# One addition over four PSUM banks in place of four: the output tiles of a steady MLP unit

## The reference, cut to what matters

```python
cms_out  = gelu(attn_out @ cW1 + cb1) @ cW2 + cb2 + target_embed      # 512 -> 2048 -> 512
concat   = concatenate([attn_out, cms_out], axis=-1)
modifier = gelu(concat @ mW1 + mb1) @ mW2 + mb2                       # 1024 -> 2048 -> 512
out      = clip(x + cms_out + modifier, 0.0, 1.0)
```

## Time and profile before

| | us |
|---|---|
| median of 3 runs | 1183.29 |
| lowest and highest of them | 1183.22, 1184.39 |
| span of the profiled execution, first to last instruction | 1181.1 |
| PE busy in it | 1150.9 (97%) |
| DVE busy | 617.0 (52%) |
| ACT busy | 348.1 (29%) |
| POOL busy | 225.0 (19%) |
| PE's granted clock, mean | 0.993 |

### The profile page before, as it was taken

One profiled execution on the slowest core, in us unless ns is written; L12 is line 12 of the kernel. 1 busy time (PEld: TensorE's weight loads), 2 busy tenths in 40 slices (PEclk: granted clock), 3 DMA queues, 4 the chain that ended last, 5 costly groups with the idle time before them and its releaser, 6 DMA issues.

```text
span 1181.1 us, 14411 instructions
## 1 busy us (share of the span) xinstructions
PE 1150.9 (97%) x5201; PEld 954.2 (81%) x5201; DVE 617.0 (52%) x943; ACT 348.1 (29%) x611; POOL 225.0 (19%) x158
## 2 busy tenths in 40 slices
PE   7999999999999999999899999999999999999993
PEld 6888888788888888888788888888888888888883
DVE  4334344266656566665963444444444444344866
ACT  4333333322232232322421221221212212213554
POOL 2303113110110110110911111101001111113355
PEclk9999999999999999999999999999999999999997
DMA  5011000000010010010000000000000000001522
GB/s 179 1 37 36 0 36 18 18 25 30 18 36 18 18 36 18 18 36 27 27 27 27 27 27 26 1 27 27 27 27 27 27 27 27 27 14 59 152 81 89
DMA packets 41671, 41.33 MB, mean 35 GB/s; under 512 B 2165, under 2 KB 28841, under 8 KB 41641
## 3 DMA queue, kind: packets, MB, share of 16 engines
q1 hardware_dynamic: 41640, 40.93, 11.0%
HBM read 36.73 MB, written 4.19 MB: 35 GB/s over the span
## 4 chain that ended last, share of the span: by engine, by line
PE 90%; DVE 4%; ACT 2%; POOL 2%; DMA 1%; issue 1%; SPq 0%; POOLq 0%; ACTq 0%; DVEq 0%
PE bank L416 30%; PE bank L418 30%; PE bank L417 30%; PE bank L428 1%; DVE stats L944 1%; POOL res L382 1%; DMA raw<-W_up_dram 0%; POOL cms_lo L351 0%; DMA Wk_raw<-Wk_dram 0%; DVE z_odd L942 0%; DVE z_even L942 0%; DVE z_even L931 0%; POOL wsplit L351 0%; ACT gelu_f L738 0%; ACT wsplit L739 0%
## 5 line engine op out<-in xcount | busy, mean ns | idle before, releaser
L861 DVE TENSOR_TENSOR res<-bank,res 128x512 f32<-128x512 f32 x240 | 163.9, 691 | 261.3 <-PE bank L418 261.3
L680 ACT ACTIVATE gelu_f<-bank,hidden_bias 128x512 f32<-128x512 f32 x128 | 88.3, 690 | 636.3 <-PE bank L418 636.1
L351 POOL TENSOR_TENSOR wsplit<-raw,wsplit 128x512 fp32r<-128x512 f32 (+1 forms) x64 | 100.8, 1576 | 717.9 <-ACT wsplit L607 717.9
L861 DVE TENSOR_TENSOR cms_acc<-bank,cms_acc 128x512 f32<-128x512 f32 x240 | 163.4, 691 | 121.7 <-PE bank L418 121.7
L416 PE MATMUL bank<-attn_hi,wsplit 128*128 128x512 f32 x512 | 200.0, 391 | 3.1 <-DVE cms_lo L868 3.1
L416 PE MATMUL bank<-gelu_hi,wsplit 128*128 128x512 f32 x512 | 199.3, 389 | 0.8 <-DVE gelu_lo L847 0.8
L418 PE MATMUL bank<-attn_hi,wsplit 128*128 128x512 f32 x512 | 199.8, 390 | 0.0
L417 PE MATMUL bank<-attn_lo,wsplit 128*128 128x512 f32 x512 | 199.8, 390 | 0.0
L418 PE MATMUL bank<-gelu_hi,wsplit 128*128 128x512 f32 x512 | 199.2, 389 | 0.0
L417 PE MATMUL bank<-gelu_lo,wsplit 128*128 128x512 f32 x512 | 199.2, 389 | 0.0
L416 PE MATMUL bank<-cms_hi,wsplit 128*128 128x512 f32 x288 | 113.2, 393 | 2.9 <-DVE z_even L942 1.8
(11 more groups left out here) (131 smaller groups left out, 1287.6 us busy)
## 6 DMA issues: line engine op xcount, KB each, us to landing
raw<-cW_dram SPq DMA_DIRECT2D x32, 256.0 KB, 2.8
raw<-mW_dram SPq DMA_DIRECT2D x16, 512.0 KB, 4.2
x_raw<-x_dram SPq DMA_DIRECT2D x4, 1024.0 KB, 5.3
raw<-mW_dram SPq DMA_DIRECT2D x16, 256.0 KB, 4.4
raw<-W_down_dram SPq DMA_DIRECT2D x4, 512.0 KB, 3.8
raw<-W_up_dram SPq DMA_DIRECT2D x4, 512.0 KB, 4.7
out_dram<-z_even SPq DMA_DIRECT2D x8, 256.0 KB, 2.0
out_dram<-z_odd SPq DMA_DIRECT2D x8, 256.0 KB, 2.0
```

What stands on the lines that cost most here:

```text
L351: pool.tensor_tensor(dst, src, f32(hi), ALU.subtract).then_inc(done, 1)
L680: act.activation(dst[:, g, :], bank[r][:, :], ACT.Gelu, bias=hidden_bias[:, s:s + 1]).then_inc(gelu_made, 1)
L861: op = dve.tensor_tensor(dst, src, dst, ALU.add)
```

## The change

The PSUM tensors `bank[4]` to `bank[7]` become one tensor `outs` of 128 x 4 x 512, of which they are now slices. A steady `add_unit` (no start of an accumulator) waits once, for the fourth output tile, and adds all four tiles with one 128x2048 instruction, which raises `summed` by 4. The first four units of each MLP keep their four instructions.

```diff
-        bank = [ctx.enter_context(nc.psum_tensor(f"bank{i}", [P, 512], F32)) for i in range(8)]
+        bank = [ctx.enter_context(nc.psum_tensor(f"bank{i}", [P, 512], F32)) for i in range(4)]
+        outs = ctx.enter_context(nc.psum_tensor("outs", [P, KT, 512], F32))
+        bank += [outs[:, m, :] for m in range(KT)]
...
             def add_unit(i, r, total, start=None):
 
+                if start is None:
+                    dve.wait_ge(out_filled, i * 4 + KT)
+                    dve.tensor_tensor(total[:, r, :, :], outs[:, :, :], total[:, r, :, :], ALU.add).then_inc(summed, KT)
+                    return
                 for m in range(KT):
                     dst, src = total[:, r, m, :], bank[4 + m][:, :]
                     dve.wait_ge(out_filled, i * 4 + (m + 1))
                     if start == "cms":
                         op = dve.tensor_scalar(dst, src, cms_bias[:, r, m:m + 1], None, ALU.add)
-                    elif start == "mod":
+                    else:
                         if m == 0:
                             dve.wait_ge(res_added, KT * (r + 1))
                         op = dve.scalar_tensor_tensor(dst, src, bias[:, MB2 + m:MB2 + m + 1], dst, ALU.add, ALU.add)
-                    else:
-                        op = dve.tensor_tensor(dst, src, dst, ALU.add)
                     op.then_inc(summed, 1)
```

## The result

The changed kernel takes 1229.4 us (median of 4 runs, 1229.2 to 1229.9) against 1183.3 us: 46.1 us slower, a ratio of 1.0383 with a 95% interval of 1.0369 to 1.0398. The forecast was 1224 us, the range 1207 to 1242. The profiled execution took 1229.2 us with a span of 1227.4, so 1.8 us lie around the span here; the forecast had taken 2.2.

What follows compares the result with a forecast made beforehand. PE was taken to bound the kernel, other engines counting only where they make it wait. Terms 34.0 + 2.8 + 2.4 + 0 + 1.6 = 40.8 us on a span of 1181.1 gave 1224 us, range 1207 to 1242.

Steps and rivals of the forecast that it cites:

- What bounds, and the chain: Whole kernel: PE bounds, busy 97% of the span; in steady cms units low(i+1) follows the addition, out(i+1) follows low(i+1).
- Part 1 and 2: Steady addition: waiting for the fourth tile loses 2.04 us of cover; one 2048-element instruction takes 2.29 us.
- Part 3: Steady cms units: each 0.43 to 0.62 us over 5.44, in sum 34.0 us up to out(60).
- Part 4: Between the MLPs: hidden(64) 2.8 us later, then 2.4 us of wait at hidden(66).
- Part 5: Mod units: nothing lost, 7.2 us of addition chain hidden within a unit of 8.16 us.
- Part 6: End of the kernel: the chain from add(126) on ends 1.6 us later.
- the clock stayed at 1.00: Rival on steady cms units: PE's clock falls after each of 56 gaps, 95 us more, 1320 us; chance 0.04.
- the addition ran at the single rate: Rival: the wide addition runs at double rate, 1.43 us, and fits the slack, 1185 us; chance 0.04.
- merging did save its fixed costs: Rival: nothing saved by merging, wide addition 2.76 us, 0.47 more in 56 units, 1250 us; chance 0.06.

Runs made afterwards that it cites:

- low-first: Changed kernel with DVE making the low part of unit i ahead of the wide addition of unit i-1 in the cms MLP: 1192.0 us, ratio 1.0065.
- four late additions: Changed kernel with its one 128x2048 addition replaced by four 128x512 additions behind the same single wait for the fourth tile: 1238.9 us, ratio 1.0466.
- the turns: Kernel before, with GpSimd's additions of batch r into res waiting until cms_lo of batch r-1 is done: 1179.9 us, ratio 0.9974; rerun 1180.0 us.
- mod-only: Changed kernel with the wide addition kept in the second (mod) MLP only, the steady cms additions narrow again: 1186.5 us, ratio 1.0019.
- changed kernel with turns: Changed kernel with GpSimd's additions of batch r into res waiting until cms_lo of batch r-1 is done: 1223.7 us, ratio 1.0344.

## Why the prediction was right, and what it sized wrongly

- **What bounds, and the chain** (fourth tile, wide addition, low part, output matmuls): right. The low-first run takes 38 us away by moving the low part out of it.
- **Part 1 and 2, the wait and the instruction:** right, 2292 ns against 2290. The four late additions show the parts separately. DVE's additions became 52 us shorter, where 56 had been estimated from the fixed cost; as foretold, that bought PE nothing.
- **Part 3, the steady unit:** this is the term that was too small, 38.5 us against 34.0. Of the 5.98 us in written-out code, 6.06 to 6.11 were measured, 0.62 to 0.67 over; of the 6.06 in the loop, 6.14, 0.70 over. Two things were missing. The wide addition starts 0.07 us later behind the last tile than a narrow one does, perhaps through its separate wait; I had carried the narrow one's 2.92 over. And out(i) behind a wait is 0.13 us longer, not 0.11, since some of the next matmuls are 0.01 late too. The 0.08 us for the wait in an instruction of its own, taken from ACT, was right: low ends at 506.49, PE starts at 506.63, 0.13 to 0.14 in the loop against 0.06 in written-out code.
- **Part 4, the passage:** 5.65 against 5.2, by chance nearer than the larger of its parts: one was 0.9 us too small and the other 0.4 too large. hidden(64) came 3.7 us later and not 2.8, because low(62) took 2.36 us and not 1.2: it fell on POOL's first split (2.4 us from 609.26), and not on its additions (low(61), started just before these, took 0.68). The later wait, at hidden(66), was 1.67 us, and out(65) came 1.97 later for it, at the full clock, against 2.4. By the turns POOL's collision with cms_lo carries roughly 1.8 us of this term; the steady loss of two more units and low(62) carry 3.
- **Part 5, the mod units:** 0.00 us.
- **Part 6, the end:** 1.8 us against 1.6; 0.07 of it is the later start again. The other 0.1 isn't traced, and is less than this stretch varies (3.0 us in the mod-only trace).
- **The rivals:** the clock stayed at 1.00 in the steady units, the addition ran at the single rate, and merging did save its fixed costs. What the prediction didn't see is that its deadline for PE was the matmul's start. In the steady unit this cost nothing in the sum, because the restart's 0.11 us was counted on its own; in low-first it cost 2.5 us. The rest of what low-first was over its 1187 us is the passage, which I had put at 0.8 to 1.8 us there and which took 5.25.

## What to carry to other kernels

An evacuation that runs tile by tile beside the matmuls has most of its time hidden; merging it into one instruction makes it wait for the last tile, and what counts then is the longest chain behind that tile, not the busy time saved (67 us less of DVE's busy time, and 46 us lost). Before merging, add up that chain and compare it with the time to the weight load of the matmul that waits. Where an independent short step stands behind the merged one on its engine, put it in front.

## What the runs showed of the hardware

- A wait for an output bank holds PE's weight load, not only the matmul: in low-first the load came at 506.80 instead of 506.68, and the unit became 0.05 us longer, though the matmul itself started in time.
- A DVE addition from PSUM starts 0.04 us behind the modelled end of the last matmul when its wait is inside it (512 elements, one bank or two), and 0.11 us when the wait is an instruction of its own (1024 and 2048 elements). Four banks in one instruction have no other cost in these runs: 2292 ns for 2048 elements, 691 for 512.
- DVE's SBUF-only subtractions and POOL's instructions slow each other while both run: cms_lo takes 1.7 us a tile beside POOL and 0.6 alone, and POOL's 128x512 additions 1.73 beside it and 1.29 alone. DVE's additions from PSUM keep 0.69 and 2.29 us beside POOL.
- After the same wait of PE, 3.12 us, the granted clock was 0.50 for some 3 us in the kernel before and 1.00 in the mod-only kernel. After 2.01 us it fell in the changed kernel; after 2.05 us at the same place in the changed kernel with turns it didn't.
